# A linear-attention and mixture layer on one core: the state product in two half-width tiles, and the loop over sequences written out

## The reference

```python
q, k, v = split(xn @ wqkv)            # 16 heads of 16 features; q and k go through relu
kv = cumsum(k[..., :, None] * v[..., None, :], axis=2)     # running state per head
num = einsum('bhnd,bhnde->bhne', q, kv)
den = einsum('bhnd,bhnd->bhn', q, cumsum(k, axis=2))[..., None] + EPS
attention = (num / den) @ wo
scores = sigmoid(xn @ Wr)             # top 2 of 8: four gated MLPs (silu(g) * u @ Wd),
mixture = routed experts + depthwise causal convolution of 4 taps over xn
```

## Time and profile before

| what | us |
|---|---|
| median of 3 runs (lowest to highest) | 1415.48 (1414.07 to 1416.15) |
| the profiled execution, whole | 1417.17 |
| its span in the trace | 1415.4 |
| PE busy | 1373.6 (97%) |
| PEld busy | 1194.5 (84%) |
| DVE busy | 1087.9 (77%) |
| POOL busy | 811.6 (57%) |
| ACT busy | 734.5 (52%) |

### The profile page before, as it was taken

The page is one execution under the profiler, slowest core; times in us unless marked ns, Lnnn a source line. Parts: engine busy times, 40 slices in busy tenths (PEclk is TensorE's granted clock), DMA queues, the critical chain, the costliest instruction groups (busy, mean ns, idle before and its releaser), DMA issues.

```text
span 1415.4 us, 55195 instructions
## 1 busy us (share of the span) xinstructions
PE 1373.6 (97%) x23392; PEld 1194.5 (84%) x23392; DVE 1087.9 (77%) x2566; ACT 734.5 (52%) x1545; POOL 811.6 (57%) x679
## 2 busy tenths in 40 slices
PE   4999999999999999999999999999999999999997
PEld 3788887888888888888888888888888888878886
DVE  5778787778787778877777877788877788867874
ACT  5455554455554455554555554455544555535551
POOL 1755665655656655656556657556556556565553
PEclk9899999999999999999999999999999999999998
DMA  5011101111111121011111011111111111101110
GB/s 168 4 63 62 62 33 33 62 62 62 47 48 32 62 62 63 32 38 56 62 63 59 35 38 56 63 62 47 47 32 63 62 62 43 51 32 47 47 47 16
DMA packets 46790, 73.86 MB, mean 52 GB/s; under 512 B 6480, under 2 KB 42192, under 8 KB 42448
## 3 DMA queue, kind: packets, MB, share of 16 engines
q1 hardware_dynamic: 46544, 70.24, 14.7%
HBM read 53.18 MB, written 17.04 MB: 50 GB/s over the span
## 4 chain that ended last, share of the span: by engine, by line
PE 95%; DVE 2%; issue 1%; SPq 1%; ACT 1%; DMA 0%; DVEq 0%; ACTq 0%
PE ring L311 48%; PE scores L311 16%; PE ring L432 9%; PE ring L422 6%; PE scores L368 5%; PE state_sum L383 4%; PE scores L321 2%; PE ring L450 2%; PE scores L350 2%; DVE sm L764 1%; DMA x_t<-in_L_attn_x_dram 0%; DVE x_t L836 0%; SPq L268 0%; DVE cT L786 0%; ACT qp L527 0%
## 5 line engine op out<-in xcount | busy, mean ns | idle before, releaser
L637 POOL TENSOR_TENSOR hid<-hid,cwb 128x512 f32<-128x512 f32 x128 | 163.1, 1275 | 217.4 <-DVE hid L794 214.6
L786 DVE SCALAR_TENSOR_TENSOR cT<-xT,conv_ws,cT 128x512 f32<-128x512 f32 x192 | 256.9, 1377 | 0.0
L625 POOL TENSOR_TENSOR x_t<-x_t,same 128x1024 f32<-128x1024 f32 x32 | 76.9, 2404 | 286.3 <-ACT same L534 286.3
L550 ACT ACTIVATE sg<-ring 128x512 f32<-128x512 f32 x128 | 76.7, 599 | 303.1 <-PE ring L311 303.1
L311 PE MATMUL ring<-xl,wgu_h 128*128 128x512 f32 x512 | 212.9, 416 | 8.7 <-DVE x_t L836 6.8
L311 PE MATMUL ring<-xh,wgu_l 128*128 128x512 f32 x512 | 203.5, 397 | 0.0
L311 PE MATMUL ring<-xh,wgu_h 128*128 128x512 f32 x512 | 202.6, 396 | 0.0
L490 ACT ACTIVATE yh<-yT 128x256 fp32r<-128x256 f32 x128 | 53.6, 418 | 286.7 <-DVE yT L807 286.7
L794 DVE TENSOR_TENSOR hid<-ring,sg 128x512 f32<-128x512 f32 x128 | 88.2, 689 | 137.4 <-PE ring L311 137.2
L641 POOL TENSOR_TENSOR hl<-hid,hh 128x512 fp32r<-128x512 f32 x128 | 193.0, 1508 | 0.0
L764 DVE TENSOR_TENSOR sm<-scores,causal_s 128x512 f32<-128x512 f32 x256 | 159.0, 684 | 29.1 <-PE scores L368 28.6
(11 more groups left out here) (110 smaller groups left out, 3591.1 us busy)
## 6 DMA issues: line engine op xcount, KB each, us to landing
cwb<-cw_rows SPq DMA_DIRECT2D x32, 1024.0 KB, 4.8
x_t<-in_L_attn_x_dram SPq DMA_DIRECT2D x32, 512.0 KB, 5.2
out_dram<-x_t SPq DMA_DIRECT2D x32, 512.0 KB, 3.0
cw_rows<-cwt SPq DMA_DIRECT2D x128, 2.0 KB, 1.4
sm<-in_L_attn_wqkv_dram SPq DMA_DIRECT2D x2, 384.0 KB, 4.9
sm<-in_L_ffn_Wg_dram SPq DMA_DIRECT2D x2, 256.0 KB, 4.7
sm<-in_L_ffn_Wu_dram SPq DMA_DIRECT2D x2, 256.0 KB, 5.4
cwb<-in_L_ffn_Wd_dram SPq DMA_DIRECT2D x1, 512.0 KB, 5.6
```

The lines of the kernel that those rows point to most:

```text
L550: act.activation(sg[:, :], GB[t % 2], ACT.Silu).then_inc(s_sg, 1)
L625: pool.tensor_tensor(xb, xb, same[:, :, :], ALU.add).then_inc(s_base1, 1)
L637: pool.tensor_tensor(hid[:, e, :], hid[:, e, :], cwb[:, e, :], ALU.mult).then_inc(s_hid, 1)
L786: ins = dve.scalar_tensor_tensor(out=cT[:, c, :], in0=xT[:, j % 2, c, n:n + BT], scalar=conv_ws[:, c, n:n + 1], in1=cT[:, c, :], op0=ALU.m ...
```

## The change

In `numerators`, each product of `state_bd` and the query becomes two, each with 64 of the 128 weight columns, writing partitions 0 to 63 or 64 to 127 of the same bank. In `rounds`, the loop goes and all 32 batches are written out on every engine, with constants as the values of all waits. `met`, `settled` and `s_met` go.

```diff
-        def rounds(engine, body):
-
-            with engine.Fori(0, n_seq - 1) as s:
+        def rounds(body):
+
+            for s in range(n_seq):
                 for j in range(BPS):
-                    body(s, j, BPS)
-            for j in range(BPS):
-                body(n_seq - 1, j, BPS - 1 - j)
+                    body(s, j, min(BPS, (n_seq - s) * BPS - 1 - j))
...
                 if not first:
                     pe.wait_ge(s_bd, chunk_at(s, j + k, n))
-                    met(pe)
...
                     pe.wait_ge(s_sg, at(s, j, T, t + 1))
-                    met(pe)
...
                         for g in range(C):
                             n0 = t * P + h * HALF
-                            ins = mm(NB2[t % 2][h][:, g * HALF:(g + 1) * HALF], state_bd[:, n % 4, g * P:(g + 1) * P],
-                                     qT[:, g, n0:n0 + HALF], start=False, stop=True, skip_group_check=True)
+                            for w in range(2):
+
+                                rows = slice(w * HALF, (w + 1) * HALF)
+                                cols = slice(g * P + w * HALF, g * P + (w + 1) * HALF)
+                                ins = mm(NB2[t % 2][h][rows, g * HALF:(g + 1) * HALF], state_bd[:, n % 4, cols],
+                                         qT[:, g, n0:n0 + HALF], start=False, stop=True, skip_group_check=True)
...
                 pool.tensor_tensor(rstd[:, :], vare[:, :], half[:, :], ALU.pow).then_inc(s_rstd, 1)
-                settled(pool)
```

More of the change, by code:

```diff
@@ L165, in layer_kernel @@
         s_own = sem("s_own")
-        s_met = sem("s_met")
         s_bn = sem("s_bn")
@@ L244, in layer_kernel @@
         OWN_BODY = 2 + OWN_HEADS
[L246 to L252, removed]
         block = ctx.enter_context(nc.Block())
@@ L300, in _ @@
             spread_cw(0, 0, 0)
-            rounds(sp, batch)
+            rounds(batch)
         @block.tensor
@@ L485, in _ @@
             pe.wait_ge(w_split, N_SPLITS)
-            rounds(pe, batch)
+            rounds(batch)
         @block.scalar
@@ L596, in _ @@
             heads(0, 0, 0)
-            rounds(act, batch)
+            rounds(batch)
         @block.gpsimd
@@ L674, in _ @@
             base(0, 0, 0)
-            rounds(pool, batch)
+            rounds(batch)
         @block.vector
@@ L865, in _ @@
             assert count["setup"] == OWN_SETUP, count
-            rounds(dve, batch)
+            rounds(batch)
 _INS = ["L0_attn_x", "L0_attn_wqkv", "L0_attn_wo", "L0_ffn_Wr", "L0_ffn_router_bias", "L0_ffn_Wg", "L0_ffn_Wu",
```

## The result

| kernel | us, median (lowest to highest) | ratio to before, 95% interval |
|---|---|---|
| before | 1415.82 (1414.07 to 1421.6) | |
| after | 1347.26 (1346.0 to 1348.11) | 0.9508 (0.9480 to 0.9537) |

The profiled execution of after took 1346.54 us with a span of 1344.8; before's was 1417.17.

A forecast was written before the change was run, and what follows sets the result against it. PE was taken to bound the kernel, L432 by loading 128 columns per 64 streamed. 1417.17 - 44.6 (blocks) - 9.1 (turns) + 1.2 (shape) + 17 (fetching) = 1381.7, less 1.7 for the profiled execution: 1380 us, range 1356 to 1416.

The forecast's parts named there:

- What bounds the kernel: Whole kernel: PE holds 95% of the chain of waits, so a microsecond off PE is one off the kernel.
- The block: State product (L432): halves run side by side, block falls from 1.04 to 0.68 us; 124 blocks gain 44.6 us.
- The first rival: State product: the two halves take turns, so the split gains nothing; 1420 us, chance 0.14.
- Change of shape: From the state product's last block to the full-width value product: 0.04 us, 31 times, 1.2 us cost.
- Turns: Six loop turns where PE's next batch starts late, blamed on the branch: 6 x 1.52 = 9.1 us gained.
- What the written-out text costs: Dense runs of small tiles in straight text: 20 issue stalls of 1.05 us less four there now, 17 us cost.
- Register arithmetic and increments: All engines: dropping register arithmetic and s_met increments priced at nothing, covered by PE's queued work and other engines' idle time.
- That the parts can be added up: Whole kernel: 1417.17 - 44.6 - 9.1 + 1.2 + 17 = 1381.7 us, 1380 us after the profiled execution's offset.
- VectorE's slack: VectorE's block diagonal state (L771), ready at 701.83, used at 702.23 after the change: 0.4 us left.

The follow-up runs named there:

- padded: The kernel after with 128 semaphore increments on PE ahead of the first batch: 1396.81 us, ratio 0.9838.
- padded_64: The kernel after with 64 semaphore increments on PE ahead of the first batch: 1368.93 us, ratio 0.9647.
- padded_192: The kernel after with 192 semaphore increments on PE ahead of the first batch: 1385.73 us, ratio 0.9762.
- before_padded: The kernel before with 128 semaphore increments on PE ahead of the loop: 1528.21 us, ratio 1.0765.
- split_in_loop: The kernel before with only the state product split in two halves; loop, register waits and increments kept: 1469.73 us, ratio 1.0345.
- straight_with_markers: The kernel after with the semaphore increments behind PE's waits put back, 14 in a batch, no loop: 1434.67 us, ratio 1.0109.
- loop_of_two: The kernel before with two sequences in the loop and six written out behind it, full-width product and increments kept: 1434.72 us, ratio 1.0108.

## Why the prediction missed, by its steps

| step | forecast, us | in the traces, us |
|---|---|---|
| block of the state product, with the change of shape | -43.4 | -48.7 |
| turns of the loop | -9.1 | -9.5 |
| fetches in the written-out text, less those of before | +17 | -4.2 |
| register arithmetic and increments | 0 | -8.2 (short gaps; up to 4.6 of it the granted clock at the start and in the tail) |
| sum | -35.5 | -70.6 |

*What bounds the kernel*: right. The chain stayed on PE and every microsecond came through.

*The block*: right in mechanism, an eighth short in size. The halves run side by side: 0.61 us against a forecast of 0.68, and the old 1.04 for halves in turn. The first rival, and with it the Trainium skill's rule (TensorE: Matmul & The Clock Gate, Part 3: Packing small matmuls), asks for different row groups for a load beside a running matmul (the same part also names the background weight buffer as a way to load ahead, which the rival left out); here both halves use all 128 rows and the block fell by 0.43 us all the same. The measurement decides: they don't take turns. In what way the loads overlap, no run here shows. A round of two pieces takes 0.062 us (forecast 0.06). The rest was too large, and partly right by luck: the old block is seven steps of 0.119 us and a way out of 0.205, not eight of 0.111 and 0.15; the new one is fifteen steps of 0.031 and a way out of 0.152, 0.617 in all. The 0.05 added for a first load that nothing hides was not there: from the numerators to the block's first multiply it is 0.146 us in both kernels.

*Change of shape*: forecast 1.2 us, measured 31 times 0.152 instead of 0.084 us ahead of the value product, 2.1 us; as small as said. Leaving the block for the state sum went the other way, from 0.205 to 0.152.

*Turns*: right, and right against the view of waits, which named VectorE's L836: in the shifted kernel the same gap stands as issue, and in the written-out ones, with the same work on VectorE, it is gone.

*What the written-out text costs*: this step failed, and it is 21 of the 35 us by which the forecast missed. It read the four stalls of the last sequence as a property of straight text, "one in two batches", and left the increments out: "the register arithmetic and the s_met increments I price at nothing". Two things set the stalls. The increments behind the waits: put back they cost 37 us in full-width text and 88 with the split, and in the text with the split most of it goes with where they stand and not with their number (66 us less when moved). The last sequence of before had them; the kernel after does not, so its four stalls were no sample of it. And the place of the packet edges: the same text shifted costs 0, 13, 31 or 10 us over its own place, 14 in the mean. Taken over places, 21 us gross was the right order; the kernel after sits, by luck, at the one of four where it is 0.

*Register arithmetic and increments, "at nothing, both ways"*: this is what put the time below the range. Its low end, 1357, already had a gain of 0.40 a block and only three stalls, nearly what was measured (0.39 and none). What it lacked is the 8.2 us of short gaps: up to 4.6 of them are the clock, for which the sum had no term, and how the rest divides between register arithmetic and increments stays open.

*That the parts can be added up*: the sum assumed it. Less the increments ahead of the first batch:

| text | own place | shifted by 128 increments |
|---|---|---|
| loop, full width (before) | 1419 | 1509 |
| loop, split | 1470 | 1390 |
| written out, full width, no increments | 1404 | 1401 |
| written out, split, no increments (after) | 1346 | 1377 |

The measured 5% is between one place of each text. In the right-hand column the same change is worth 131 us, and the split alone in the loop 119 instead of -50. The split's own work is about 49 us (before against after); what varies is stalls and the half clock behind some of them. Part of what a shift adds is clock too: behind the increments of padded, padded_64 and padded_192 PE stays at half clock for 4 to 6 us more. Text without loop and increments varies least: 1346, 1356, 1359 and 1377 over the four places.

*VectorE's slack*: 0.4 us forecast ahead of the state sum, 0.33 measured; no wait came up.

## What to carry to other kernels

Where an engine runs through hundreds of small instructions in a few microseconds, its instruction fetch belongs in the sum: look for idle time put down to issue inside dense runs, keep semaphore instructions from between a wait and such a run, and before an edit of some per cent is believed run both versions shifted by part of a packet, since a difference between two placements is not the edit's worth. Look at the granted clock of each version as well: a stall can be followed by a stretch at half clock that no row of waits shows. A full-width tile that streams only 64 columns was bound here by its load; cut in two column halves its pieces took little more than half the time even though both halves use all the rows.

## What the runs showed that I had not expected

- An increment of a semaphore on PE takes 0.149 to 0.153 us when many stand in a row (9.5, 19.4 and 29.3 us for 64, 128 and 192).
- Shifting an unchanged program by half a packet moved its time by +89 us (loop, full width) and -80 us (loop, split).
- In every stall behind the start-up of padded, padded_64, padded_192, before_padded, split_in_loop, straight_with_markers and loop_of_two a packet lands 1.2 to 1.7 us before PE goes on (102.84 and 104.10 in padded); the transfer itself takes 0.9 to 1.5 in padded.
- Behind a stall the granted clock can fall to half: 16 times in before_padded, never in the kernel after.
- A loop of two turns ahead of 1300 us of straight text left no trace in it (1345.8 against 1346.2).
- A turn of the long loop costs 1.5 to 1.9 us in one placement and 2.0 to 2.8 in another.
